# Weighing and summing eight experts: one multiply-add per expert on VectorE, or wide products on VectorE and sums on GpSimd

## The reference

```
gate    = softmax(h @ gate_w + gate_b)                  # 8 experts
weights = gate * (gate >= 0.1);  weights /= sum(weights)
out     = sum over e of weights[e] * (h @ expert_w[e] + expert_b[e])
x       = x + out
```

## Time and profile before

| | us |
|---|---|
| median of 3 runs | 2001.14 (2000.14 to 2002.01) |
| the profiled execution's own time | 2003.77 |
| its span in the trace | 2001.9 |
| TensorE, VectorE, ScalarE, GpSimd busy | 1563.9, 1733.1, 1599.4, 1501.7 |
| of VectorE's: the 256 multiply-adds of L1168 | 68.5 |

### The profile page before, as it was taken

How to read it: one execution, slowest core, us unless ns; L and a number is a source line. 1 busy time by engine, 2 the same in 40 slices (tenths; PEclk the granted TensorE clock), 3 DMA queues, 4 the chain that set the end, 5 groups by cost and what they waited for, 6 DMA issues and landing times. The chain is left out here.

```text
span 2001.9 us, 26596 instructions
## 1 busy us (share of the span) xinstructions
PE 1563.9 (78%) x8451; PEld 555.9 (28%) x8579; DVE 1733.1 (87%) x3742; ACT 1599.4 (80%) x1374; POOL 1501.7 (75%) x1026
## 2 busy tenths in 40 slices
PE   3778787877888878878887888888887687899966
PEld 1122222212222222222222222222221244466655
DVE  5889999998999999989999999999997488755556
ACT  2789999999999999999999999999999211222243
POOL 4899999998999999899999999999997001000010
PEclk7789999999999999999999999999999787877778
DMA  3110000000000000010000000000000000000001
GB/s 87 40 44 13 14 18 13 13 13 29 28 13 14 18 13 13 13 44 13 13 13 17 15 13 13 14 17 13 13 13 7 1 1 0 1 0 1 1 0 43
DMA packets 32491, 33.12 MB, mean 17 GB/s; under 512 B 5657, under 2 KB 23136, under 8 KB 32352
## 3 DMA queue, kind: packets, MB, share of 16 engines
q1 hardware_dynamic: 30117, 30.12, 4.9%
q10 hardware_dynamic: 2235, 1.28, 0.3%
HBM read 22.74 MB, written 8.39 MB: 16 GB/s over the span
## 5 line engine op out<-in xcount | busy, mean ns | idle before, releaser
L905 POOL TENSOR_TENSOR sigma_weights<-grown 128x1024 f32<-128x1024 f32 x480 | 911.8, 1903 | 0.0
L594 DVE TENSOR_SCALAR sigma_weights<-ps_sig 128x512 int32<-128x512 int32 x1024 | 690.3, 674 | 62.0 <-PE ps_sig L431 60.9
L813 ACT ACTIVATE tau_weights<-ps_tau 128x1024 f32<-128x1024 f32 x506 | 706.6, 1396 | 29.4 <-PE ps_tau L443 29.4
L799 ACT ACTIVATE sigma_weights<-sigma_weights,kernel_shape 128x2048 f32<-128x2048 f32 x256 | 608.0, 2375 | 27.6 <-POOL sigma_weights L905 27.6
L603 DVE TENSOR_TENSOR running_max<-ps_sig,running_max 128x512 f32<-128x512 f32 x896 | 604.1, 674 | 0.0
L878 POOL TENSOR_SCALAR grown<-sigma_weights,kernel_shape 128x1024 f32<-128x1024 f32 x480 | 542.6, 1130 | 60.3 <-DVE sigma_weights L594 59.6
L808 ACT ACTIVATE sigma_weights<-sigma_weights 128x2048 f32<-128x2048 f32 x256 | 586.0, 2289 | 0.1
L485 PE MATMUL ps_acc<-tau_weights,v_heads 128*9 128x512 f32 x2048 | 533.8, 600 | 3.8 <-ACT sigma_weights L808 2.2
L485 PE MATMUL ps_acc<-sigma_weights,v_heads 128*9 128x512 f32 x2048 | 536.7, 603 | 0.0
L443 PE MATMUL ps_tau<-q_operand,k_operand 128*128 128x512 bf16 x885 | 278.7, 385 | 217.2 <-ACT tau_weights L813 209.2
L431 PE MATMUL ps_sig<-q_operand,k_operand 96*128 96x512 bf16 x1024 | 402.0, 393 | 57.0 <-DVE running_max L603 33.2
(11 more groups left out here) (172 smaller groups left out, 1444.3 us busy)
## 6 DMA issues: line engine op xcount, KB each, us to landing
q_operand<-q_parts SPq DMA_DIRECT2D x192, 48.0 KB
k_operand<-k_parts SPq DMA_DIRECT2D x63, 144.0 KB
q_parts<-parts SPq DMA_DIRECT2D x24, 128.0 KB, 2.3
k_parts<-parts SPq DMA_DIRECT2D x18, 128.0 KB, 2.3
x_res<-in_L_attn_x SPq DMA_DIRECT2D x8, 256.0 KB, 4.7
q_operand<-max_rows SPq DMA_DIRECT2D x128, 2.0 KB
out<-x_res SPq DMA_DIRECT2D x4, 512.0 KB, 3.2
k_parts<-parts ACTq DMA_DIRECT2D x6, 128.0 KB, 2.7
```

Source lines behind the costliest of these rows:

```text
L594: dve.tensor_scalar(sig[:, g % SIG_RING, cols].bitcast(I32), ps_sig[:, half, :].bitcast(I32), SIGN_OFF, None, ALU.bitwise_and).then_inc(ma ...
L799: act.activation(chunk(c), chunk(c), ACT.Ln, bias=shape[:, CHUNK * c // TB % H, 1:2]).then_inc(ln_done, 1)
L813: act.activation(tau[:, g % TAU_RING, :], (ps_tau, ps_sig)[tau_bank(g)[0]][:, :, :].rearrange("p h q -> p (h q)"), ACT.Exp, scale=float(DH ...
L905: pool.tensor_tensor(sig[:, g % SIG_RING, :], t, t, ALU.mult).then_inc(sq_ready, 1)
```

## The change

VectorE multiplies four experts of a tile at once, 512 columns from PSUM, by their four weights, each repeated over 128 columns, and writes the products to a new buffer in SBUF, `weighed`, with two halves for two pairs. GpSimd adds the eight products of both tiles of a pair in three steps (1024, 512 and 256 columns out) and adds the result to x in a fourth (256 columns). It waits for the bias add before the fourth. VectorE waits, before a pair's first product, for the sums of the pair two before (the same half of the buffer); the waits between its operations and the one ahead of the bias add go. GpSimd's order for batch b is: sums of pairs 0 and 1, the norm of b+1, sums of pairs 2 and 3. PSUM banks come free after each half's two products.

```diff
--- before.py
+++ after.py
@@ -972,6 +972,7 @@
         guard = sb("gate_guard", [P, TB])
         weight = sb("gate_weight", [P, TB, E])
         weight_t = sb("gate_weight_t", [E, N])
+        weighed = sb("weighed", [P, 2, 2, 2, 4, D])
         ps_t = ctx.enter_context(nc.psum_tensor("ps_mt", [P, 2, HALF], F32))
         ps_y = ctx.enter_context(nc.psum_tensor("ps_my", [P, 2, HALF], F32))
         ps_e = ctx.enter_context(nc.psum_tensor("ps_me", [P, 2, 2, HALF], F32))
@@ -983,7 +984,9 @@
         yn_ready, x_step, x_ready, z_ready = sem("yn_ready"), sem("x_step"), sem("m_x_ready"), sem("m_z_ready")
         gate_ready, gate_step, exp_ready = sem("gate_ready"), sem("gate_step"), sem("gate_exp")
         bias_ready, bias_added = sem("expert_bias_ready"), sem("expert_bias_added")
-        e_ready, e_step = sem("e_ready"), sem("e_step")
+        e_ready, e_step, e_summed = sem("e_ready"), sem("e_step"), sem("e_summed")
+
+        PAIR, PAIRS_OF = 4, TB // 2
         GATE = 11
         block = ctx.enter_context(nc.Block())
 
@@ -1053,7 +1056,7 @@
 
                     for half in range(2):
 
-                        wait(pe, e_step, b * TB * E + max(0, 2 * E * (pair - 1) + E * (half + 1)))
+                        wait(pe, e_step, b * PAIRS_OF * PAIR + max(0, PAIR * (pair - 1) + 2 * (half + 1)))
                         for t in (2 * pair, 2 * pair + 1):
                             pe.matmul(ps_e[:, t % 2, half, :], turned_sb[:, 1, t * P:(t + 1) * P],
                                       w["experts"][:, 4 * half:4 * half + 4, :], start=True, stop=True).then_inc(e_ready, 1)
@@ -1080,8 +1083,7 @@
 
                 return rows[:, :].unsqueeze(1).to_broadcast([P, TB, D])
 
-            for b in range(B):
-
+            def norm(b):
                 xs = w["x"][:, bass.ds(b * TB, TB), :]
                 pool.wait_ge(yn_ready, b * TB + TB)
                 pool.wait_ge(x_ready, b)
@@ -1090,6 +1092,23 @@
                 pool.wait_ge(x_step, b + 1)
                 alone(pool, w["pool_passed"])
                 pool.tensor_tensor(xs, xs, yn[:, :, :], ALU.add).then_inc(x_ready, 1)
+
+            def sums(pair):
+                def part(b):
+                    n = b * PAIRS_OF + pair
+                    terms, xs = weighed[:, pair % 2], w["x"][:, b * TB + 2 * pair:b * TB + 2 * pair + 2, :]
+                    pool.wait_ge(e_step, PAIR * n + PAIR)
+                    pool.tensor_tensor(terms[:, 0], terms[:, 0], terms[:, 1], ALU.add).then_inc(e_summed, 1)
+                    pool.wait_ge(e_summed, 4 * n + 1)
+                    pool.tensor_tensor(terms[:, 0, :, 0:2, :], terms[:, 0, :, 0:2, :], terms[:, 0, :, 2:4, :], ALU.add).then_inc(e_summed, 1)
+                    pool.wait_ge(e_summed, 4 * n + 2)
+                    pool.tensor_tensor(terms[:, 0, :, 0, :], terms[:, 0, :, 0, :], terms[:, 0, :, 1, :], ALU.add).then_inc(e_summed, 1)
+                    pool.wait_ge(e_summed, 4 * n + 3)
+                    pool.wait_ge(bias_added, b * 2 + 2)
+                    pool.tensor_tensor(xs, xs, terms[:, 0, :, 0, :], ALU.add).then_inc(e_summed, 1)
+                return part
+
+            rounds(pool, [(0, sums(0)), (0, sums(1)), (1, norm), (0, sums(2)), (0, sums(3))])
 
         @block.vector
         def _(dve):
@@ -1156,24 +1175,19 @@
             def experts(pair):
                 def part(b):
 
-                    done = 2 * E * pair
-                    if pair == 1:
-                        dve.wait_ge(bias_added, b * 2 + 2)
-                    for e in range(E):
+                    n = b * PAIRS_OF + pair
+                    wait(dve, e_summed, 4 * (n - 1))
+                    for half in range(2):
                         for t in (2 * pair, 2 * pair + 1):
-                            if e > 0:
-                                dve.wait_ge(e_step, b * TB * E + (done - 1))
-                            if e % 4 == 0:
-                                dve.wait_ge(e_ready, b * 2 * TB + (4 * pair + 2 * (e // 4) + t % 2 + 1))
-                            dve.scalar_tensor_tensor(out=xt(b, t), in0=ps_e[:, t % 2, e // 4, (e % 4) * D:(e % 4 + 1) * D],
-                                                     scalar=weight[:, t, e:e + 1], in1=xt(b, t),
-                                                     op0=ALU.mult, op1=ALU.add).then_inc(e_step, 1)
-                            done += 1
+                            dve.wait_ge(e_ready, b * 2 * TB + (4 * pair + 2 * half + t % 2 + 1))
+                            dve.tensor_tensor(weighed[:, pair % 2, half, t % 2, :, :],
+                                              ps_e[:, t % 2, half, :].rearrange("p (e d) -> p e d", e=4),
+                                              weight[:, t, 4 * half:4 * half + 4].unsqueeze(2).to_broadcast([P, 4, D]),
+                                              ALU.mult).then_inc(e_step, 1)
                 return part
 
             def biases(b):
 
-                dve.wait_ge(e_step, b * TB * E + 2 * E)
                 for g in range(2):
                     dve.wait_ge(bias_ready, b * TB + 4 * (g + 1))
                     xs = w["x"][:, bass.ds(b * TB + 4 * g, 4), :]
```

## The result

The changed kernel takes 2010.18 us (median of 6, 2007.54 to 2010.80), the kernel before 2001.43 in the same series (median of 6). The ratio is 1.0041 with a 95% interval of 1.0030 to 1.0052: slower by 8.2 us, by more than 0.2%. The profiled execution took 2010.80 us; its span is 2009.0, 7.1 more than before.

The account below looks back on a forecast made before the run. In each round only VectorE's pair 3 was taken as on the path, the other pairs covered by TensorE or GpSimd's norm. Tail +7.4, products -5.1, held z +4.2 gave +6.5: 2007.6 us, range 2002.4 to 2011.5.

Parts of the forecast that it names:

- The tail: In the last batch nothing covers GpSimd's sums, at 5.6 us a pair, so the stage ends 7.4 us later.
- T: The moment when a batch's last pair of tiles (pair 3) is done; the forecast counts its times from there.
- Products: VectorE's four wide products take 2.5 us a pair against 4.22; only pair 3 gains, -5.1 us in three rounds.
- z held: Pair 2's sums on GpSimd hold z's eight VectorE tensor-scalars by 0.64 to 2.1 us, taken as 1.4: +4.2 us in three rounds.
- The gate held: Pair 3's sums hold VectorE's gate until T+6.0 in place of T+2.95, hidden because TensorE reaches the weights at T+6.59: cost 0.
- The rounds: One batch's last experts to the next one's: 37 us, nearly as before, from -1.7 for pair 3 and +1.4 for z.
- it ends 0.3 us after TensorE's gate products, so they don't cap it: Shortened pair 3 ends at 1665.74, after TensorE's gate products at 1665.45, so its 1.7 us gain a round stays.
- Rival 3: TensorE's clock stays at 1.00, pair 0's matmuls take 3.70 us instead of 6.61; gate not held: -6.4 us, 1994.7, chance 0.05.
- The sum: Whole kernel: tail, pair 3's gain and held z together make it 6.5 us slower, 2007.6 us; chance 0.58.

Follow-up runs that it names:

- e1: The changed kernel with its last batch the old way (16 multiply-adds a pair on VectorE, no sums): median 2002.9 us, ratio 1.0002 to the kernel before.
- e9: The kernel before plus four GpSimd adds on a scratch buffer behind each norm but the first, awaited by nobody: median 1995.0 us, ratio 0.9969.
- e6: As e1, but GpSimd begins the sums of pair 3 only after the next batch's gate: median 2003.1 us, ratio 1.0004 to the kernel before.
- e2: The changed kernel, but GpSimd begins pair 2's sums only when the next batch's z is made: median 2016.2 us, ratio 1.0066 to the kernel before.
- e3: The changed kernel with the edits of both e1 and e2: median 2000.4 us, ratio 0.9985 to the kernel before.
- e5: Only pair 3 of the first three batches the new way, all else as the kernel before: median 1987.5 us, ratio 0.9925.
- e7: As e6, and GpSimd waits for z after the first add of pair 2's sums: median 1988.7 us, ratio 0.9931 to the kernel before.
- e12: The kernel before plus one useless 512-column GpSimd multiply at the end of the expert stage: median 1994.9 us, ratio 0.9968.

## Why the prediction was right, and where it was not

The forecast was +6.5 us and slower; the profiled execution has +7.1 and the runs +8.2, inside the range.

- **The tail.** Predicted from T to the end +7.4. Measured: T is 1704.76 and the end 1735.62, 30.86 us against 24.16, so +6.7. The three sums began at T+15.1, 0.5 us later than forecast. The adds were priced right (2.35, 1.27, 0.72); the 0.18 us between dependent ones was too much, it was 0.07 to 0.08: a pair takes 5.25 us, not 5.6. e1 takes the tail away and with it 6.3 us.
- **Products.** Predicted 2.5 us a pair, measured 2.47. Pairs 0 and 2 were hidden as said. The stride-0 operand costs nothing.
- **z held.** Predicted 0.64 to 2.1 us, taken as 1.4; measured 1.2, and e9 shows it with no other change. GpSimd's last adds did both get in between, but began earlier than I had put them. The rule of the Trainium skill (SBUF — State Buffer, "Who interferes with whom") held here for the three kinds that occur: two SBUF inputs held (0.50 us for 0.22), a tensor-scalar from SBUF to SBUF held (3.34 for 2.14), one input in PSUM not (2.48 for four products).
- **The gate held.** Predicted to be hidden by TensorE, with the cover named. It was; it ended at 1635.26, TensorE came at 1636.79. e6 frees it, and nothing that shows is gained by that. Where the cover goes (e2, e3, e5: TensorE waits 0.5 to 2.2 us for the weights), the hold shows at once.
- **The rounds.** By my terms each should take 0.3 us less. Between the ends of pair 3 they took 37.74 and 37.65 us against 37.70 and 37.38; the first, from the gate to the end of pair 3, took 36.3 against 37.0. The step that failed is "it ends 0.3 us after TensorE's gate products, so they don't cap it". I took 1.91 us for them from the old trace and kept the clock that went with it. In the changed kernel they ran at 0.50, took 3.52 us and did cap it. So pair 3's gain was lost in two places, of which I had one. That the held z lowers this clock isn't shown: e3 has 3.52 us behind a free z, e9 has 1.91 behind a held one.
- **Rival 3.** Its mechanism is real, and half as large as put there: without holds pair 0's matmuls take 5.40 us, neither 6.61 nor 3.70. I had capped it with the held gate, which was right for the change as made.
- **The sum.** From the first gate to the end of the last sum the stage took 142.57 us against 136.23: +6.3. The two misses, 0.7 us too much for the tail and 0.5 too little for the rounds, nearly cancel by luck, and some 0.7 us more lies before the first gate and behind the stage. Beyond that the runs can't be read to a microsecond: "behind" alone can move by 10 us, and it happened to stay at 186 here.

## What to carry to other kernels

A summing engine that looks idle is free only where nothing else needs its way to SBUF and where its last piece is covered: look for VectorE operations with two SBUF inputs, or tensor-scalars from SBUF to SBUF, beside it, put its pieces around them, and give the last batch the old path. Here the same new work in another order, with the old path for the last batch (e7), makes the stage 8.7 us shorter than before, where the change made it 7.0 longer; three pairs alone (e5) bring 4.6.

When two versions differ by a few microseconds, compare the windows of the parts that neither of them edits before you believe in an edit: a jump there is no merit of the edit, and a delay of one operation tests it.

## What the runs showed of the hardware that was not expected

- The causal attention takes 176 or 186 us with the same instructions, by when its start falls against the rise of TensorE's granted clock (14 profiles); a useless 1.3 us operation in front makes the kernel 0.32% faster (e12).
- VectorE and GpSimd take turns operation by operation: with four adds in a row on GpSimd, z got in one operation between each two (3.34 us against 2.14), and a gate operation waited for a whole add (2.27 us for 0.22).
- What the gate's 8-column matmuls cost isn't set by the work alone: 1.91 us at 1.00, 3.52 at 0.50, and either behind a held z or a free one (e3, e9).
- Statistics from one SBUF input took 1.65 us for eight beside the running sums (at 1620.52 in the changed kernel), as beside an idle GpSimd.
- Two GpSimd adds where the second needs the first's result start 0.07 us apart from its end; in the norm, where GpSimd also raises a semaphore between the two, it is 0.18.
